# Feed-forward weights stored tile by tile, and large tiles at multiples of 512 bytes, in a transformer layer on one core

## What is computed

```python
def block(x):
    x = x + attn(layernorm(x))     # q, k, v = h @ Wq, Wk, Wv; rope on q and k; causal softmax; (probs @ v) @ Wo
    x = x + ffn(layernorm(x))      # (silu(h @ W_gate.T) * (h @ W_up.T)) @ W_down.T
    return x
```

## Time and profile before

| | us |
|---|---|
| median of three runs | 799.4 (798.14 to 801.4) |
| the profiled execution | 799.8 |
| its span, first to last instruction | 798.1 |
| TensorE busy with matmuls | 763.0 (96%), 4240 of them |
| VectorE busy | 441.1 (55%) |
| ScalarE busy | 341.8 (43%) |
| GpSimd busy | 211.5 (27%) |

### The profile page before, as it was taken

How to read it: one execution, slowest core, us unless ns; L and a number is a source line. 1 busy time by engine, 2 the same in 40 slices (tenths; PEclk the granted TensorE clock), 3 DMA queues, 4 the chain that set the end, 5 groups by cost and what they waited for, 6 DMA issues and landing times.

```text
span 798.1 us, 12148 instructions
## 1 busy us (share of the span) xinstructions
PE 763.0 (96%) x4240; PEld 507.8 (64%) x4240; DVE 441.1 (55%) x984; ACT 341.8 (43%) x684; POOL 211.5 (27%) x384
## 2 busy tenths in 40 slices
PE   4699999999999997999799999999999999999998
PEld 3545444554444443454588888888878888788886
DVE  7787878788877786996445543233322243231212
ACT  3427767766876776668533222111121111121111
POOL 3326763577446753234300000000000000000000
PEclk9959999999999999899999999999999999999999
DMA  7437777234423436370286101412005120030001
GB/s 263 110 89 247 211 239 217 68 85 121 117 78 100 121 100 197 113 209 27 92 252 181 56 14 52 132 42 65 27 1 168 43 79 26 0 106 0 1 1 53
DMA packets 74613, 81.84 MB, mean 103 GB/s; under 512 B 8720, under 2 KB 58384, under 8 KB 74352
## 3 DMA queue, kind: packets, MB, share of 16 engines
q1 hardware_dynamic: 73264, 79.98, 32.8%
q10 hardware_dynamic: 1296, 1.18, 0.6%
HBM read 57.02 MB, written 33.36 MB: 113 GB/s over the span
## 4 chain that ended last, share of the span: by engine, by line
PE 50%; DVE 0%; issue 0%; DVEq 0%
PE bank L1495 35%; PE ps_y L1547 15%; PE bank L1534 1%; DVE x_in L1477 0%; DVEq L1476 0%
## 5 line engine op out<-in xcount | busy, mean ns | idle before, releaser
L734 ACT ACTIVATE probs<-ps_t 128x512 f32<-128x512 f32 (+1 forms) x352 | 184.2, 562 | 89.9 <-PE ps_t L1145 89.6
L869 DVE CUSTOM_DVE_ANT_0 ps_s<-ps_s,mask_row 128x512 f32<-128x512 f32 (+1 forms) x240 | 145.4, 643 | 42.4 <-PE ps_s L1113 41.2
L1113 PE MATMUL ps_s<-k_rows,q_rows 96*128 96x256 bf16 (+3 forms) x512 | 146.8, 316 | 5.7 <-DMA q_rows<-scratch_q_parts 3.7
L1452 DVE TENSOR_TENSOR h<-h,bank 128x512 f32<-128x512 f32 (+1 forms) x44 | 30.3, 688 | 218.9 <-PE bank L1495 217.7
L1145 PE MATMUL ps_t<-q_rows,k_rows 98*128 98x512 bf16 (+1 forms) x352 | 129.4, 371 | 7.3 <-DMA q_rows<-m_t 4.5
L1390 ACT ACTIVATE h<-bank 128x512 f32<-128x512 f32 (+1 forms) x44 | 26.3, 599 | 149.3 <-PE bank L1495 149.3
L642 POOL TENSOR_SCALAR_AFFINE_SELECT probs<-probs 128x512 f32<-128x512 f32 x128 | 84.4, 659 | 0.0
L873 DVE TENSOR_REDUCE m_raw<-ps_s 128x2 f32<-128x512 f32 (+3 forms) x112 | 73.2, 677 | 19.7 <-PE ps_s L1118 19.2
L1158 PE MATMUL ps_o<-probs,v_ones 128*32 128x512 f32 (+3 forms) x1024 | 82.6, 441 | 0.2 <-ACT o_sb L744 0.2
L1396 ACT CAST h_hi<-h 128x512 fp32r<-128x512 f32 (+1 forms) x44 | 27.3, 621 | 128.4 <-DVE h L1452 128.4
L223 POOL TENSOR_TENSOR var_eps<-mean_var,eps 128x1 f32<-128x1 f32 x16 | 3.1, 191 | 289.6 <-DVE mean_var L218 289.6
(11 more groups left out here) (154 smaller groups left out, 1380.6 us busy)
## 6 DMA issues: line engine op xcount, KB each, us to landing
scratch_o<-o_sb SPq DMA_DIRECT2D x31, 256.0 KB, 2.3
q_rows<-scratch_q_parts SPq DMA_DIRECT2D x32, 192.0 KB
x_in<-in_x SPq DMA_DIRECT2D x16, 256.0 KB, 4.6
q_rows<-scratch_q_parts SPq DMA_DIRECT2D x32, 128.0 KB
x_res<-in_x SPq DMA_DIRECT2D x16, 256.0 KB, 2.7
o_in<-scratch_o SPq DMA_DIRECT2D x64, 64.0 KB
inverse<-scratch_inverse SPq DMA_DIRECT2D x64, 64.0 KB
out<-x_in SPq DMA_DIRECT2D x16, 256.0 KB, 2.1
```

What stands on the lines that cost most here:

```text
L734: nc.scalar.activation(probs[:, g % 2, heads * u:heads * (u + 1), CHUNK_AT[c]:CHUNK_AT[c + 1]], ps_t[:, pos % S_BANKS, 0:heads * CHUNK_N[c ...
L869: nc.vector.tensor_tensor_reduce(out=bank, in0=bank, in1=mask_row[:, T - width:T], scale=1.0, scalar=LOWEST, op0=ALU.add, op1=ALU.max, acc ...
L1113: mm = nc.tensor.matmul(bank[:, place], q_rows[r][0:ROWS, j, P * q:P * (q + 1)], k_rows[r][0:ROWS, 0:width], start=(place == 0), stop=mask ...
L1452: nc.vector.tensor_tensor(h[0:m, r], h[0:m, r], bank[units["up", f] % BANKS][0:m, :], ALU.mult).then_inc(h_ready, 1)
```

## The change

`wg` and `wu` become flat, [128, 3968], and a tile f of them is one stretch of 4 x 128 (the last: 4 x 96) numbers, the 4 chunks one behind the other; the new helper `ffn_tile` cuts it out. The loads, the splits and the operands of the matmuls go through it. Rows of a tile are then 512 bytes apart (384 in tile 10).

A tile `front` of 384 bytes before all others brings `wo` to a multiple of 512, and a tile `behind` of 320 bytes fills up after the six small ones, so what either phase places next starts at a multiple of 512 again. In phase 1 the tiles of other sizes (`ident_b`, `m_raw`, `m_parts`, `m_t`, `stats`, `mean_var`, `var_eps`, `rstd`, `carrier`) are declared behind the large ones. No instruction is added, taken away or moved in its queue.

```diff
@@ Handover
+        sb("front", [P, 96])
         self.wo = [sb(f"wo_{p}", [P, KC, D], F32R) for p in ("hi", "lo")]
...
         self.rstd = sb("rstd2", [P, 1])
+        sb("behind", [P, 80])
@@ phase_1
-        ident_b = sb("ident_b", [P, P], BF16)
         mask_q = sb("mask_q", [P, GROUP, P], BF16)
...
-        stats = sb("stats", [P, TT, 6])
-        mean_var = sb("mean_var", [P, TT, 2])
-        var_eps = sb("var_eps", [P, TT])
-        rstd = sb("rstd", [P, TT])
-        carrier = sb("carrier", [P, 2, TT])
...
+        probs = sb("probs", [P, 2, GROUP, CHUNK_AT[TT]])
+        o_sb = sb("o_sb", [P, 2, T])
+        sums = sb("sums", [P, P])
+        ident_b = sb("ident_b", [P, P], BF16)
         m_raw = sb("m_raw", [P, 2, TT * GROUP])
         m_parts = sb("m_parts", [P, 2, 2, GROUP, TT], BF16)
         m_t = [sb(f"m_t{r}", [2 * GROUP * TT, P], BF16) for r in range(2)]
-        probs = sb("probs", [P, 2, GROUP, CHUNK_AT[TT]])
-        o_sb = sb("o_sb", [P, 2, T])
-        sums = sb("sums", [P, P])
+        stats = sb("stats", [P, TT, 6])
+        mean_var = sb("mean_var", [P, TT, 2])
+        var_eps = sb("var_eps", [P, TT])
+        rstd = sb("rstd", [P, TT])
+        carrier = sb("carrier", [P, 2, TT])
@@ phase_2
-        wg = [sb(f"wg_{p}", [P, KC, F - FIRST * P], F32R) for p in ("hi", "lo")]
-        wu = [sb(f"wu_{p}", [P, KC, F - FIRST * P], F32R) for p in ("hi", "lo")]
+        wg = [sb(f"wg_{p}", [P, KC * (F - FIRST * P)], F32R) for p in ("hi", "lo")]
+        wu = [sb(f"wu_{p}", [P, KC * (F - FIRST * P)], F32R) for p in ("hi", "lo")]
...
+        def ffn_tile(w, f):
+            at = KC * P * (f - FIRST)
+            return w[:, at:at + KC * FW[f]].rearrange("p (c n) -> p c n", c=KC)
+
         def gate_weights(part, c, f):
             if f < FIRST:
                 return to.w[part][:, c, P * f:P * (f + 1)]
-            return wg[part][:, c, P * (f - FIRST):P * (f - FIRST) + FW[f]]
+            return ffn_tile(wg[part], f)[:, c, :]
...
-                    sp.dma_start(w[1][:, :, at:at + m].bitcast(F32),
+                    sp.dma_start(ffn_tile(w[1], f).bitcast(F32),
...
-                    nc.scalar.copy(w[0][:, :, at:at + m], w[1][:, :, at:at + m].bitcast(F32)).then_inc(ffn_hi_ready, 1)
+                    nc.scalar.copy(ffn_tile(w[0], f), ffn_tile(w[1], f).bitcast(F32)).then_inc(ffn_hi_ready, 1)
...
-                    nc.vector.tensor_tensor(w[1][:, :, at:at + m], w[1][:, :, at:at + m].bitcast(F32),
-                                            w[0][:, :, at:at + m].bitcast(F32), ALU.subtract).then_inc(ffn_split, 1)
+                    nc.vector.tensor_tensor(ffn_tile(w[1], f), ffn_tile(w[1], f).bitcast(F32),
+                                            ffn_tile(w[0], f).bitcast(F32), ALU.subtract).then_inc(ffn_split, 1)
```

More of the change, by code:

```diff
@@ L1283, in up_weights @@
                 return to.w[part][:, c, P * (FIRST + f):P * (FIRST + f + 1)]
-            return wu[part][:, c, P * (f - FIRST):P * (f - FIRST) + FW[f]]
+            return ffn_tile(wu[part], f)[:, c, :]
         def splits(f):
@@ L1303, in load_ffn @@
             def load_ffn(f):
-                m, at = FW[f], P * (f - FIRST)
+                m = FW[f]
                 for w, name in ((wg, "wg_raw"), (wu, "wu_raw")) if f >= FIRST else ():
-                    sp.dma_start(w[1][:, :, at:at + m].bitcast(F32),
+                    sp.dma_start(ffn_tile(w[1], f).bitcast(F32),
                                  d[name].rearrange("(c p) n -> p c n", p=P)[:, :, P * f:P * f + m]
```

## The result

Eight runs of the changed kernel have a median of **793.1 us** (791.6 to 796.5), and eight of the kernel before, beside them, 799.1 us: a ratio of 0.9935 (0.9918 to 0.9951). In a later set of runs it was 792.1 against 799.1 us, 0.9908 (0.9877 to 0.9939). The profiled execution took 795.1 us, with a span of 793.4 us and a mean granted clock of 0.978.

A forecast was written before the change was run, and what follows sets the result against it. Phase 2 was taken as bound by TensorE's matmul pitch. From the profiled 799.8 us, 5.7 (phase 2) and 0.6 (attention) off gave 793.5; with the runs' median 0.4 lower, 793.1 us, range 789.0 to 798.6.

The forecast's parts named there:

- one term of 0.6 us: Attention: moving its tiles to multiples of 512 gains 0.6 us, between 2.5 us gained and 2.5 us lost.
- The term of phase 2: Feed-forward and output projection matmuls: agreeing remainders bring them to 226.7 ns, a gain of 5.7 us over four batches.
- One sign: Start of a phase 2 batch: if `w`'s 48 matmuls take other than 10.88 us, the absolute remainder counts.
- The reason: TensorE's weight and moving-data reads fall into step when remainders modulo 512 agree, 226.7 ns, against 232.5 when they change.
- Down projections as victims: Down projections of tiles 2 to 8, slowed behind tiles 3 to 9, go from 2.77 to 2.72 us: 0.35 a batch.
- Tile 10: Last feed-forward tile, 96 columns: keeps rows of 384 bytes with changing remainders, so its 0.11 us a batch stays.
- The sign for it: Profile after the change: attention ends at 390 to 391 us if the forecast is right.
- What stood beside the forecast: Attention's 4.1 us wait for the transfer of `m_t`: if it went, 4 to 9 us would go with it.
- No effect: Rival for the whole kernel: addresses play no part in the pitch, time stays 799.4 us; chance 0.10.
- Row length alone: Rival: only row length of `wg` and `wu` mattered; tiles 3 to 9 gain 3.9 us, 795.5 us; chance 0.08.
- Remainder 0 better than other equal pairs: Rival in phase 2: 226.7 ns is not the floor, 12 us more gained, 781 us; chance 0.07.
- worse: Rival: remainder 0 locks matmuls into the pitch of tiles 3 to 9, slower, 805.5 us; chance 0.05.

The follow-up runs named there:

- the rows of 4096 bytes: The kernel before with the six small tiles ahead of `wo`, all large tiles at remainder 320, and `wg` alone in rows of 4096 bytes: 796.1 us.
- a later experiment: The kernel before with only the transfer of `m_t` put ahead of the ten loads it was issued behind: 799.7 us, ratio 1.0001.

## Why the prediction was right

*Time.* 793.1 us was forecast and 793.1 measured. So close is luck, since the runs of one kernel are spread over 5 us and one term of 0.6 us was wrong: the medians lie 6.1 us apart, phase 2 gives 5.7 of that, and the rest is within the spread. The forecast stands on its terms.

*The term of phase 2 held:* 5.7 forecast, 5.67 measured. Its parts did too: 24 of tiles 3 to 9 in 5.44 us, down in 2.72, the batches at 102.6, the settling at the start at 11.14 instead of 11.15. One sign seems to speak against it: `w`'s 48 matmuls take 10.91 us and not 10.88, which was to mean that the absolute remainder counts. It doesn't: they take 10.91 with everything at 128 as well, where `w` and `xt` lie at the remainder of before. By the starts, the first five of the 48 are slow (233, 235, 229, 232, 231 ns), at remainders 0, 128 and 320 alike; in the kernel before only the first is (229). Why is open; it costs 0.03 us a batch.

*The reason held in its core and was wrong in two details.* That operands that agree give 226.7 ns is shown by each run: flat tiles at a constant difference were slow, places alone left `wg` and `wu` slow, everything at 128 was as quick as everything at 0. But the text said that the streams are "thrown out of step when they change". They needn't change, each constant difference that was run, 32 to 224 bytes, costs 2 to 7 ns a matmul. And the period is 256 bytes, not the 512 that the rows were read by. By that table the output projection's middle value in the kernel before falls in place: 320 against 128 is 192, the mildest difference measured, while the weights of `wg` and `wu` went between 192 and 64. In what way the two read streams disturb each other is not shown; the runs show only that the pitch follows the difference.

*Down projections as victims* were assumed (0.35 us a batch); the places alone and the rows of 4096 bytes show it, with the floor reached again after four and seven matmuls.

*Tile 10* kept its cost as forecast (0.11 us a batch forecast, 0.12 measured), for a reason that was mostly another: about 60% of its gate's share goes with the 96 columns and stays with rows that agree.

*The term of attention failed:* 0.6 us forecast, nothing found. The triple and what follows it, against the earlier trace rows:

```profile
161.64 0.40 PE L1068 MATMUL ps_d<-xt_lo,w_hi 128*128 128x512 f32 x1
161.87 0.40 PE L1068 MATMUL ps_d<-xt_hi,w_lo 128*128 128x512 f32 x1
162.11 0.39 PE L1148 MATMUL ps_t<-q_rows,k_rows 98*128 98x512 bf16 x1
162.34 0.38 PE L1116 MATMUL ps_s<-k_rows,q_rows 96*128 96x512 bf16 x1
```

They keep the distances of before, 0.23, 0.24, 0.23. The bf16 matmuls' other places, old or new, are worth nothing. The row's own argument, that the interruption stays, should have led to nought. The sign for it, attention's end at 390 to 391 us, failed too: it came at 392.2 and 386.5 us in two profiles of the changed kernel, by the wait for `m_t` and the first 60 us.

*What stood beside the forecast*, the wait for `m_t`, was sized well (4 to 9 us if it went): 6.4 us were won in its place with the transfer put first. It differs between executions and is a part, at least, of what spreads the runs. That its price would simply be saved was the theory of a later experiment and fell: 1.0001.

*The rivals.* No effect: excluded by the interval. The Trainium skill ("SBUF — State Buffer", section "Who interferes with whom") has the two read ports independent and TensorE waiting on no one; the runs disagree on the first, since with the same instructions in the same order the distance of the two operands' addresses alone moves the pitch from 226.7 to 233 ns. Row length alone: flat tiles alone gain 0.46 us a batch and not the 0.98 of that rival, nor the 1.44 of the whole. Remainder 0 better than other equal pairs, or worse: neither, 128 and 320 are the same to 1 ns.

## What to carry to other kernels

Where a run of float32 matmuls with a new weight load under each is slower than its neighbours of the same shape, compare the addresses of the stationary and of the moving operand modulo 256 bytes: equal is the floor, and it needs neither a particular remainder nor a particular storage, only row lengths and tile sizes that are multiples of 256 bytes (by the period; all that were run are multiples of 512), and small tiles kept out from between large ones. It was worth 1 to 3% of such a stretch here, for some hundred bytes of each partition. And before a wait is paid for by reordering a queue, look for the next waiter on that queue: here the delay moved on 42 us and its price came back.

## What was not expected of the hardware

- The pitch depends on the difference with a sign: 192 bytes (228.9 ns) is milder than 64 (232.5 to 233.2).
- The weight load doesn't take longer in the slow case. In the kernel before, then in the changed one, ns min/median/max:

```profile
L1495 PEld LDWEIGHTS bank<-xt_hi,wg_hi x128: 161/188/189, 412.9 to 785.5; 128*128 128x128 f32 x112, 128*96 128x96 f32 x16
```

```profile
L1504 PEld LDWEIGHTS bank<-xt_hi,wg_hi x128: 161/188/188, 413.8 to 780.9; 128*128 128x128 f32 x112, 128*96 128x96 f32 x16
```

  It is 188 ns by either. So the 6 ns are lost between the loads or on the moving side; what in the chip couples the two reads is not shown.
- Products whose own operands agree can still disturb each other. In the kernel before, with `w` and `xt` at 128 and `h` and `wd` at 320, the down projections of tiles 0 and 1 take 2.73 us and tile 2's 24 matmuls, behind one of them, 5.48; where all four lie at one remainder it is 2.72 and 5.44. Against this stands the start of a batch, where `w`'s 48 matmuls take 10.88 us in the kernel before and 10.91 at one remainder. Neither was tested by itself.
- A weight load of 96 columns is shorter (161 ns against 188), and yet the matmuls with it are further apart: 230.0 ns at equal remainders, against 226.7.
- A slip outlives its cause: operands that agree need three to ten matmuls to come back to 226.7 ns after ones that didn't.
